# VectorE adds a chunk's residuals before it takes the pair output of the same round

## The chip, the cores and the metric

The kernel runs on one core of a Trainium2 chip. The metric is the device time of one execution in microseconds (us). The engines have short names in the profile: PE is TensorE (PEld its weight load), DVE is VectorE, ACT is ScalarE, POOL is GpSimd, SP is the engine whose queue issues the DMAs.

## What is computed

32 images of 512 channels and 48 x 48 pixels pass through two layers with residuals. Cut to what matters:

```
f     = relu(Wc @ gn(x) + bc)                  # 512 -> 128 channels       (stage A)
dynW  = kernels made per image from means and maxima of gn(x)
y     = conv3x3(f, dynW[n]) + b_ad             # 128 -> 128 channels       (stage B)
x1    = x + (Wf @ y + bf)                      # 128 -> 512 channels       (stage C)
out   = x1 + grouped_conv3x3(gn(x1), kernels)  # 32 groups of 16 channels  (stage D)
```

`gn` normalizes each of 32 groups of 16 channels. All products are made from a high and a low part of each operand, as three matmuls (`high*high`, `high*low`, `low*high`; lines 853, 854, 855).

## The kernel before, in words

Every engine runs its own list of instructions, in an order written out by hand, and semaphores tie the lists together. The unit of the lists is the step: one image n, for which stages A, B and C run, together with stage D of the image before, n - 1. Image 0 has no D beside it, and after image 31 the D of the last image runs alone. Images 2 to 29 run in a loop.

In a step TensorE makes stage A (tile `pac`), then stage B (`pb`), and then 16 rounds, r = 0 to 15. In each round it makes one pair of groups of D (`d_pair`: 18 matmuls into `pd` for even r, into `pb` for odd r). In rounds 0, 4, 8 and 11 (`C_AT`) it then makes one chunk of C: 128 of the 512 channels, as six units (`c_unit`) of three matmuls, each unit into one of three PSUM banks of `pac`. Between some rounds stand small matmuls for the statistics of the next image: the group mean (L908) behind round 7, the group variance (L912) behind round 9, and the inputs of the dynamic kernels (L920) behind round 11. The release rules of TensorE that the change touches are two lines:

```
if u >= C_BANKS: pe.wait_ge(x1_done, n * CUNITS + u - C_BANKS + 1)    # c_unit u: residual u - 3 is done
reached(pe, out_done, n * PAIRS + p - 1)                              # d_pair p: output p - 2 is taken
```

VectorE has two operations that read these results. `residual` (L764, one for each unit, writes `x1b`) adds bias and x to a unit and so frees its bank; with its sum it is two instructions, the main one and a DVE_READ_ACCUMULATOR. `output` (L774, one for each pair, writes `big`) scales the pair and adds x1. The first residual of a chunk also waits until the chunk before has been written out (`x1_out`) and until ScalarE has squared it (`sq_done`, L464), since `x1b` holds one chunk. In between VectorE works on the next image: moments (L604) in rounds 3 and 4, maxima (L612) in round 5, means (L622, L624) in round 6, variances (L630 to L638) in round 8, scales and scaled weights (L650 to L655) in round 10, their high and low parts (L659, L661) in round 11.

SP stores a quarter of an image's result once four outputs are there: `store` of chunk c of D waits for output 4c + 3, so that of chunk 2 waits for output 11. In the SP queue it stands ahead of the write of C's chunk 3 and of a load of x.

Of the kernel before, what the change touches and what calls it, by code (L numbers as in the profile page):

```python
# [81 lines left out]
def x_slot(c, odd):  # L82

    return c if c < 1 else c + 3 * odd
# [12 lines left out]
def build(nc, x, wct, bc, kks_in, wrow_in, b_ad, wft, bf, kt, out):  # L97
# [7 lines left out]
    with ExitStack() as ctx:  # L105
# [142 lines left out]
        def t_slot(c):  # L248
            return tb[:, T_SLOT[c], :, :, :]
# [9 lines left out]
        def pair_banks(p):  # L259

            return pb if p % 2 else pd


        def reached(eng, semaphore, value):

            if not isinstance(value, int) or value > 0:
                eng.wait_ge(semaphore, value)
# [273 lines left out]
        def _(vec):  # L541
# [135 lines left out]
            def x1_group_means(n):  # L677

                vec.wait_ge(stat_mm2, 2 * n + 1)
                reached(vec, behind_out, n * 16)  # L680
                reached(vec, ahead_out, n * 16)
                vec.tensor_scalar(mrow[:, :, :], ps[:, 32:32 + Q].unsqueeze(2).to_broadcast([P, Q, W]), -1.0, None,
                                  ALU.mult).then_inc(mrow_done, 1)
                vec.tensor_tensor(vb[:, 1, :], ps[:, 32:32 + Q], nmean[:, :], ALU.subtract).then_inc(dve_stat, 1)
                vec.wait_ge(dve_stat, STAT_LINKS * n + 2)
                vec.tensor_tensor(vb[:, 2, :], vb[:, 1, :], vb[:, 1, :], ALU.mult).then_inc(dve_stat, 1)

                vec.wait_ge(cen_done, (n + 1) * Q)
                vec.tensor_tensor(vb[:, 3, :], cen[:, :], nmean[:, :], ALU.subtract).then_inc(dve_stat, 1)
                vec.wait_ge(dve_stat, STAT_LINKS * n + 4)  # L690
                vec.tensor_tensor(vb[:, 3, :], vb[:, 3, :], vb[:, 3, :], ALU.mult).then_inc(dve_stat, 1)
                vec.wait_ge(dve_stat, STAT_LINKS * n + 5)
                vec.tensor_tensor(vb[:, 2, :], vb[:, 2, :], vb[:, 3, :], ALU.subtract).then_inc(dve_stat, 1)

            def x1_variances(n):

                vec.wait_ge(sq_done, (n + 1) * Q)
                vec.wait_ge(dve_stat, STAT_LINKS * n + 6)
                vec.scalar_tensor_tensor(out=vb[:, 0, :], in0=m2[:, :], scalar=1.0 / PX, in1=vb[:, 2, :],
                                         op0=ALU.mult, op1=ALU.add).then_inc(var_done, 1)  # L700
                vec.wait_ge(var_done, n + 1)
                mask = ind8[:, :].unsqueeze(1).to_broadcast([P, Q, GQ])
                vec.tensor_tensor(spread[:, 0], nmean[:, :].unsqueeze(2).to_broadcast([P, Q, GQ]), mask, ALU.mult)
                vec.tensor_tensor(spread[:, 1], vb[:, 0, :].unsqueeze(2).to_broadcast([P, Q, GQ]), mask,
                                  ALU.mult).then_inc(stat_ready2, 1)
# [24 lines left out]
            def x_low(n, odd, i):  # L730
                t, c = divmod(i, Q)
                r0, nr = TILES[t]
                vec.wait_ge(xs_hi, n * UNITS + i + 1)
                vec.scalar_tensor_tensor(out=xs_at(1, i, nr * W), in0=xb[:, x_slot(c, odd), r0 * W:(r0 + nr) * W],  # L734
                                         scalar=negm[:, c:c + 1], in1=f32(xs_at(0, i, nr * W)),
                                         op0=ALU.add, op1=ALU.subtract).then_inc(xs_lo, 1)

            def f_low(n, t):
                r0, nr = TILES[t]
                vec.wait_ge(f_hi, n * NT + t + 1)  # L740
                if t == 0:
                    reached(vec, sq_done, n * Q)
                vec.scalar_tensor_tensor(out=fl[:, r0 + 1:r0 + 1 + nr, 1:W + 1],
                                         in0=pac[:, t % 2, 0:nr * W].rearrange("p (r w) -> p r w", w=W), scalar=0.0,
                                         in1=f32(fh[:, r0 + 1:r0 + 1 + nr, 1:W + 1]), op0=ALU.max,
                                         op1=ALU.subtract).then_inc(f_lo, 1)
# [7 lines left out]
            def residual(n, odd, u):  # L754

                c, k = divmod(u, OR_)
                if k == 0:
                    if c == 0:
                        reached(vec, x1_out[Q - 1], n * 16)
                    else:  # L760
                        vec.wait_ge(x1_out[c - 1], (n + 1) * 16)
                    reached(vec, sq_done, n * Q + c)
                vec.wait_ge(c_mm, n * CUNITS + u + 1)
                vec.scalar_tensor_tensor(  # L764
                    out=x1b[:, c % X1_SLOTS, k, :].rearrange("p (b w) -> p b w", w=W),
                    in0=pac[:, u % C_BANKS, 0:BW].rearrange("p (b w) -> p b w", w=W), scalar=bfc[:, c:c + 1],
                    in1=xb[:, x_slot(c, odd), :].rearrange("p (b k w) -> p k b w", k=OR_, w=W)[:, k],
                    op0=ALU.add, op1=ALU.add, accum_out=sums[:, c, k:k + 1]).then_inc(x1_done, 1)

            def output(n, p):  # L770
                vec.wait_ge(d_mm, n * G + 2 * (p + 1))
                at = 2 * p % GQ
                dst = t_slot(p // PER_CHUNK)[0:M6, at:at + 2].rearrange("p j b w -> p j (b w)")
                vec.scalar_tensor_tensor(out=dst, in0=pair_banks(p)[0:M6, :, 0:BW], scalar=kout[0:M6, 2:3], in1=dst,  # L774
                                         op0=ALU.mult, op1=ALU.add).then_inc(out_done, 1)

            def step(n, odd, d=True, more=True):
                for t in range(NT):
                    for i in range(t * Q, (t + 1) * Q):
                        if i >= AHEAD:  # L780
                            x_low(n, odd, i)
                    if t:
                        f_low(n, t - 1)
                f_low(n, NT - 1)
                if d:
                    x1_group_means(n - 1)
                    x1_variances(n - 1)
                y_low(n, 0)
                for t in range(1, NT):
                    if t == SCALES_BEFORE and d:  # L790
                        for i in range(SCALE_STEPS):
                            x1_scales(n - 1, i)
                    if more and t <= len(STATS_IN_B):
                        moments(n + 1, 1 - odd, STATS_IN_B[t - 1])
                        maxima(n + 1, 1 - odd, STATS_IN_B[t - 1])
                    y_low(n, t)
                for r in range(PAIRS):
                    if d:
                        output(n - 1, r)
                    if r in C_AT:  # L800
                        for u in range(C_AT[r] * OR_, (C_AT[r] + 1) * OR_):
                            residual(n, odd, u)
                    if more and r in MOMENTS_AT:
                        c, part = MOMENTS_AT[r]
                        moments(n + 1, 1 - odd, c, range(part * BANDS, (part + 1) * BANDS))
                    if more and r in MAXIMA_AT:
                        maxima(n + 1, 1 - odd, MAXIMA_AT[r])
                    if more:
                        if r == PREP_MEANS_AT:
                            prep_means(n + 1)  # L810
                        if r == PREP_VARIANCES_AT:
                            prep_variances(n + 1)
                    if r == X1_SUMS_AT:
                        x1_means(n)
                    if more:
                        if r == PREP_SCALED_AT:
                            prep_scaled(n + 1, 0)
                            prep_scaled(n + 1, 1)
                        if r == PREP_SCALED_AT + 1:
                            prep_scaled(n + 1, 2)  # L820
                        for i in X_LOW_AT.get(r, ()):
                            x_low(n + 1, 1 - odd, i)
                        if r == DYN_LOW_AT:
                            dyn_low(n + 1)
# [204 lines left out]
```

## Time and profile before

| | |
|---|---|
| median of 3 runs | 3608.88 us (3607.25 to 3609.89) |
| profiled execution, its own time | 3609.87 us |
| its span, first to last instruction | 3608.1 us |
| PE busy | 3491.4 us, 97% |
| PEld busy | 2787.4 us, 77% |
| DVE busy | 2531.3 us, 70% |
| ACT busy | 2108.8 us, 58% |
| POOL busy | 965.9 us, 27% |
| DMA | mean 185 GB/s |

Busy time is a share of the span. A matmul's duration in the trace is longer than the distance to the next one, since matmuls are pipelined; the pace of TensorE is read from the start times. The chain of work tells which engine the end of the program waited for, step by step.

### The profile page before, as it was taken

To read this page: it belongs to the slowest core of one execution; us is meant where nothing else is said; L and a number is where in the kernel's file an instruction comes from. 1 tells how busy PE (TensorE), PEld (TensorE's weight loads), DVE (VectorE), ACT (ScalarE), POOL (GpSimd) and SP (SyncE) were. 2 spreads that over 40 slices of the span, in tenths; PEclk is the share of its full clock that TensorE was granted. 3 is DMA by queue.
4 is the path that set the end of the run, shared out by engine and by line. 5 is a ranking of instruction groups with operands and counts; after the bars stand their busy time and mean duration, and the time that the engine had idled before them with its cause. 6 is when DMAs were issued, how large, how long until landed. Compare 5 with 4: busy or idle time off the path is not lost.

```text
span 3608.1 us, 60228 instructions
## 1 busy us (share of the span) xinstructions
PE 3491.4 (97%) x18688; PEld 2787.4 (77%) x18688; DVE 2531.3 (70%) x5365; ACT 2108.8 (58%) x3559; POOL 965.9 (27%) x1039
## 2 busy tenths in 40 slices
PE   5799999999999999999999999999999999999996
PEld 4677877777877778877778777778777778777785
DVE  7666777776777777777677777767777767676642
ACT  4365555675555665655655556655556655556654
POOL 2033222232222232222332222332222322222323
PEclk9899999999999999999999999999999999999998
DMA  5567767677767677767677777677676677676666
GB/s 122 147 190 189 191 183 181 204 198 191 184 183 192 193 186 195 188 186 195 187 187 191 192 180 202 195 190 191 175 189 198 193 193 189 179 197 190 167 156 157
DMA packets 317577, 666.88 MB, mean 185 GB/s; under 512 B 58863, under 2 KB 288242, under 8 KB 288645
## 3 DMA queue, kind: packets, MB, share of 16 engines
q1 hardware_dynamic: 317317, 663.34, 68.9%
q8 instruction: 172, 2.82, 0.3%
q14 instruction: 88, 0.72, 0.1%
HBM read 355.00 MB, written 308.28 MB: 184 GB/s over the span
## 4 chain that ended last, share of the span: by engine, by line
PE 88%; issue 6%; DVE 4%; DMA 1%; DVEq 0%; POOL 0%; ACT 0%; SPq 0%; POOLq 0%; ACTq 0%
PE pb L853 15%; PE pb L855 15%; PE pb L854 15%; PE pd L853 7%; PE pd L855 7%; PE pd L854 7%; PE pac L853 7%; PE pac L854 6%; PE pac L855 6%; PE pac L927 2%; DVE x1b L764 1%; PE pac L862 1%; PE ps L920 1%; DMA big<-x 0%; DVE big L774 0%
## 5 line engine op out<-in xcount | busy, mean ns | idle before, releaser
L407 POOL TENSOR_TENSOR hl<-un,hl 128x384 f16<-128x384 f32 x1024 | 938.3, 916 | 2562.9 <-ACT hl L432 2559.8
L432 ACT ACTIVATE hl<-un 128x384 f16<-128x384 f32 x1024 | 539.1, 526 | 433.3 <-PE pb L855 363.2
L428 ACT ACTIVATE un<-big,b_t,s_t 128x384 f32<-128x384 f32 x1024 | 709.8, 693 | 15.4 <-DMA big<-x_rows 15.4
L853 PE MATMUL pb<-fh,dynh 128*128 128x480 f32 (+3 forms) x1440 | 543.7, 378 | 0.0
L854 PE MATMUL pb<-fl,dynh 128*128 128x480 f32 (+3 forms) x1440 | 541.0, 376 | 0.0
L855 PE MATMUL pb<-fh,dynl 128*128 128x480 f32 (+3 forms) x1440 | 540.7, 375 | 0.0
L774 DVE SCALAR_TENSOR_TENSOR big<-pd,kout,big 96x768 f32<-96x768 f32 x256 | 258.8, 1011 | 383.8 <-PE pd L855 383.8
L853 PE MATMUL pd<-hl,k_h 128*96 128x376 f16 (+1 forms) x1536 | 508.9, 331 | 18.1 <-POOL hl L407 18.1
L774 DVE SCALAR_TENSOR_TENSOR big<-pb,kout,big 96x768 f32<-96x768 f32 x256 | 258.8, 1011 | 355.1 <-PE pb L855 355.1
L854 PE MATMUL pd<-hl,k_h 128*96 128x376 f16 (+1 forms) x1536 | 506.7, 330 | 0.0
L853 PE MATMUL pb<-hl,k_h 128*96 128x376 f16 (+1 forms) x1536 | 506.7, 330 | 0.0
L855 PE MATMUL pd<-hl,k_l 128*96 128x376 f16 (+1 forms) x1536 | 506.6, 330 | 0.0
L855 PE MATMUL pb<-hl,k_l 128*96 128x376 f16 (+1 forms) x1536 | 505.8, 329 | 0.0
L854 PE MATMUL pb<-hl,k_h 128*96 128x376 f16 (+1 forms) x1536 | 505.7, 329 | 0.0
L454 ACT ACTIVATE xs<-pb,badc 128x480 fp32r<-128x480 f32 (+1 forms) x160 | 103.4, 646 | 658.8 <-PE pb L855 658.8
L442 ACT ACTIVATE xs<-big,negm 128x480 fp32r<-128x480 f32 (+1 forms) x640 | 397.0, 672 | 82.1 <-PE pac L855 81.0
L734 DVE SCALAR_TENSOR_TENSOR xs<-big,negm,xs 128x480 fp32r<-128x480 f32 (+1 forms) x640 | 436.4, 734 | 9.7 <-ACT xs L442 9.7
L764 DVE SCALAR_TENSOR_TENSOR x1b<-pac,bfc,big 128x384 f32<-128x384 f32 x768 | 422.4, 607 | 6.4 <-PE pac L855 6.0
L604 DVE BATCH_NORM_STATS2 bst<-big 128x6 f32<-128x384 f32 x768 | 367.3, 543 | 9.5 <-DMA big<-x 9.5
L612 DVE TENSOR_REDUCE mx<-big 128x3 f32<-128x768 f32 x384 | 339.8, 939 | 0.0
L853 PE MATMUL pac<-xs,wfh 128*128 128x384 f32 x768 | 295.6, 385 | 37.2 <-DVE x1b L764 28.7
L855 PEld LDWEIGHTS pb<-fh,dynl 128*128 128x128 f32 x1440 | 271.0, 188 | 41.7
(115 smaller groups left out, 5243.4 us busy)
## 6 DMA issues: line engine op xcount, KB each, us to landing
big<-x SPq DMA_DIRECT2D x128, 1152.0 KB, 9.8
x_rows<-x1b SPq DMA_DIRECT2D x128, 1152.0 KB, 5.6
big<-x_rows SPq DMA_DIRECT2D x128, 1152.0 KB, 12.6
out<-big SPq DMA_DIRECT2D x128, 1152.0 KB, 6.2
big<-x_rows SPq DMA_DIRECT2D x256, 192.0 KB, 13.1
x_rows<-mrow SPq DMA_DIRECT2D x64, 96.0 KB, 1.9
big<-kt SPq DMA_DIRECT2D x4, 288.0 KB, 10.7
big<-kt SPq DMA_DIRECT2D x2, 192.0 KB, 11.1
```

What stands on the lines that cost most here:

```text
L407: pool.tensor_tensor(hl[:, g % HL_RING, 1, :, 1:W + 1], un[:, g % U_RING], hl[:, g % HL_RING, 0, :, 1:W + 1], ALU.subtract).then_inc(hl_lo, 1)
L428: act.activation(un[:, g % U_RING], t_slot(g // GQ)[:, g % GQ], ACT.Identity, bias=b_t[:, g:g + 1], scale=s_t[:, g:g + 1]).then_inc(u_done, 1)
L432: act.activation(hl[:, g % HL_RING, 0, :, 1:W + 1], un[:, g % U_RING], ACT.Copy).then_inc(hl_hi, 1)
L442: act.activation(xs_at(0, i, nr * W), xb[:, x_slot(c, odd), r0 * W:(r0 + nr) * W], ACT.Identity, bias=negm[:, c:c + 1]).then_inc(xs_hi, 1)
L604: ins = vec.bn_stats(bst[:, c, i, :], xb[:, x_slot(c, odd), i * HALF:(i + 1) * HALF])
L612: ins = vec.tensor_reduce(mx[:, c, 3 * band:3 * band + 3], src.rearrange("p (r l w) -> p l r w", r=CELL, l=3), AX.XY, ALU.max)
L734: vec.scalar_tensor_tensor(out=xs_at(1, i, nr * W), in0=xb[:, x_slot(c, odd), r0 * W:(r0 + nr) * W], scalar=negm[:, c:c + 1], in1=f32(xs_a ...
L764: vec.scalar_tensor_tensor(out=x1b[:, c % X1_SLOTS, k, :].rearrange("p (b w) -> p b w", w=W), in0=pac[:, u % C_BANKS, 0:BW].rearrange("p ( ...
L774: vec.scalar_tensor_tensor(out=dst, in0=pair_banks(p)[0:M6, :, 0:BW], scalar=kout[0:M6, 2:3], in1=dst, op0=ALU.mult, op1=ALU.add).then_inc ...
L853: pe.matmul(acc, high_w, high_x, start=start, stop=False)
L854: pe.matmul(acc, high_w, low_x, start=False, stop=False)
L855: return pe.matmul(acc, low_w, high_x, start=False, stop=stop)
```

## The change

The two blocks of VectorE's rounds change places. In rounds 0, 4, 8 and 11 VectorE now does the six residuals of the chunk first and the output of the pair behind them. In the other rounds nothing changes, and the lists of TensorE, ScalarE, GpSimd and SP are the same as before.

```
                 for r in range(PAIRS):
-                    if d:
-                        output(n - 1, r)
                     if r in C_AT:
                         for u in range(C_AT[r] * OR_, (C_AT[r] + 1) * OR_):
                             residual(n, odd, u)
+                    if d:
+                        output(n - 1, r)
                     if more and r in MOMENTS_AT:
```

The first place is VectorE in round 11, behind the scaled weights (`wcs`) of round 10. `x1b<-pac` is a residual, `big<-pb` and `big<-pd` are outputs.

```order
 L598 SCALAR_TENSOR_TENSOR va<-va 128x4
 L655 TENSOR_TENSOR wcs<-wc,va 128x512
-L774 SCALAR_TENSOR_TENSOR big<-pb,kout,big 96x768
-L764 SCALAR_TENSOR_TENSOR x1b,sums<-pac,bfc,big 128x384 x6
+L764 SCALAR_TENSOR_TENSOR x1b,sums<-pac,bfc,big 128x384 x6
+L774 SCALAR_TENSOR_TENSOR big<-pb,kout,big 96x768
 L659 CAST wch<-wcs 128x512
 L661 TENSOR_TENSOR wcl<-wcs,wch 128x512
```

Output 11 has moved behind the six residuals of chunk 3; the high and low weights behind them stay where they were.

The second place is VectorE from round 3 to round 6, with the chunk of round 4 and the statistics behind it. Before:

```order
L604 BN_STATS bst<-big 128x6 x3
L774 SCALAR_TENSOR_TENSOR big<-pd,kout,big 96x768
L764 SCALAR_TENSOR_TENSOR x1b,sums<-pac,bfc,big 128x384 x6
L604 BN_STATS bst<-big 128x6 x3
L774 SCALAR_TENSOR_TENSOR big<-pb,kout,big 96x768
L612 TENSOR_REDUCE mx<-big 128x3 x3
L774 SCALAR_TENSOR_TENSOR big<-pd,kout,big 96x768
L622 COPY cent<-mx 128x4x9
L624 BN_AGGR mv<-bst 128x2 x4
```

And with the change:

```order
L604 BN_STATS bst<-big 128x6 x3
L764 SCALAR_TENSOR_TENSOR x1b,sums<-pac,bfc,big 128x384 x6
L774 SCALAR_TENSOR_TENSOR big<-pd,kout,big 96x768
L604 BN_STATS bst<-big 128x6 x3
L774 SCALAR_TENSOR_TENSOR big<-pb,kout,big 96x768
L612 TENSOR_REDUCE mx<-big 128x3 x3
L774 SCALAR_TENSOR_TENSOR big<-pd,kout,big 96x768
L622 COPY cent<-mx 128x4x9
L624 BN_AGGR mv<-bst 128x2 x4
```

Output 4 now stands behind the residuals and ahead of the moments of round 4; everything from there on keeps its order. Rounds 0 and 8 change in the same way.

## Rows read from the trace of the kernel before

**Rows 1.** The page: span, TensorE, and granted clock in 40 slices

```profile
span 3608.1 us, 60228 instructions
...
PE 3491.4 (97%) x18688; PEld 2787.4 (77%) x18688; DVE 2531.3 (70%) x5365; ACT 2108.8 (58%) x3559; POOL 965.9 (27%) x1039
...
PEclk9899999999999999999999999999999999999998
```

**Rows 2.** The page: chain that ended last, by engine

```profile
PE 88%; issue 6%; DVE 4%; DMA 1%; DVEq 0%; POOL 0%; ACT 0%; SPq 0%; POOLq 0%; ACTq 0%
```

**Rows 3.** Waits between 130 and 3420 us: total us, times, longest us

```profile
PEld pac L853 <- DVE x1b L764: 62.7, 120, 2.9
...
PE pac L853 <- DVE x1b L764: 19.1, 32, 2.6
```

**Rows 4.** Timeline, chunk of round 0, image 14: start us, us, instruction

```profile
1610.64 0.47 PE L853 MATMUL pac<-xs,wfh 128*128 128x384 f32 x1
...
1610.98 1.01 DVE L774 SCALAR_TENSOR_TENSOR big<-pd,kout,big 96x768 f32<-96x768 f32 x1 [1.75 <-PE pd L855]
...
1611.12 0.34 PE L855 MATMUL pac<-xs,wfl 128*128 128x384 f32 x1
...
1611.83 0.34 PE L853 MATMUL pac<-xs,wfh 128*128 128x384 f32 x1
...
1611.91 0.60 DVE L764 SCALAR_TENSOR_TENSOR x1b<-pac,bfc,big 128x384 f32<-128x384 f32 x1
...
1612.45 0.61 DVE L764 SCALAR_TENSOR_TENSOR x1b<-pac,bfc,big 128x384 f32<-128x384 f32 x1
...
1612.58 0.19 PEld L853 LDWEIGHTS pac<-xs,wfh 128*128 128x128 f32 x1 [0.38 <-DVE x1b L764]
...
1613.21 0.34 PE L853 MATMUL pac<-xs,wfh 128*128 128x384 f32 x1
...
1614.29 0.33 PE L853 MATMUL pb<-hl,k_h 128*96 128x384 f16 x1
...
1617.26 0.33 PE L853 MATMUL pd<-hl,k_h 128*96 128x384 f16 x1
```

**Rows 5.** Timeline, chunk of round 11, image 14

```profile
1653.90 1.27 DVE L655 TENSOR_TENSOR wcs<-wc,va 128x512 f32<-128x512 f32 x1
...
1654.28 0.47 PE L853 MATMUL pac<-xs,wfh 128*128 128x384 f32 x1
...
1655.10 1.00 DVE L774 SCALAR_TENSOR_TENSOR big<-pb,kout,big 96x768 f32<-96x768 f32 x1
...
1655.46 0.34 PE L853 MATMUL pac<-xs,wfh 128*128 128x384 f32 x1
...
1656.02 0.60 DVE L764 SCALAR_TENSOR_TENSOR x1b<-pac,bfc,big 128x384 f32<-128x384 f32 x1
...
1656.69 0.19 PEld L853 LDWEIGHTS pac<-xs,wfh 128*128 128x128 f32 x1 [0.86 <-DVE x1b L764]
```

**Rows 6.** Timeline, chunk of round 0, image 30, and the next pair

```profile
3361.55 0.45 PE L853 MATMUL pac<-xs,wfh 128*128 128x384 f32 x1 [1.79 <-DVE xs L751]
...
3362.48 0.62 DVE L764 SCALAR_TENSOR_TENSOR x1b<-pac,bfc,big 128x384 f32<-128x384 f32 x1
...
3364.86 0.33 PE L853 MATMUL pb<-hl,k_h 128*96 128x384 f16 x1
```

**Rows 7.** Timeline, rounds 4 to 7, image 14

```profile
1626.41 1.01 DVE L774 SCALAR_TENSOR_TENSOR big<-pd,kout,big 96x768 f32<-96x768 f32 x1 [0.58 <-PE pd L855]
...
1632.91 1.01 DVE L774 SCALAR_TENSOR_TENSOR big<-pb,kout,big 96x768 f32<-96x768 f32 x1 [0.87 <-PE pb L855]
...
1637.67 0.83 DVE L624 BATCH_NORM_AGGREGATE mv<-bst 128x2 f32<-128x36 f32 x4
...
1638.67 0.28 PE L908 MATMUL ps<-mv,ind 128*128 128x4 f32 x2
```

**Rows 8.** Timeline of ScalarE: the square between rounds 9 and 11, image 14

```profile
1647.71 2.23 ACT L464 ACTIVATE fl<-x1b,cen 128x2304 fp32r<-128x2304 f32 x1
```

More of the change, by code:

```diff
@@ L797, in step @@
                 for r in range(PAIRS):
-                    if d:
-                        output(n - 1, r)
                     if r in C_AT:
@@ L802, in step @@
                             residual(n, odd, u)
+                    if d:
+                        output(n - 1, r)
                     if more and r in MOMENTS_AT:
```

## The prediction

> **What bounds the kernel now.** I read the page first. TensorE is busy for 97% of the span, the granted clock stands in its upper tenths throughout [rows 1], and the chain that ended last is 88% TensorE, against 4% VectorE [rows 2]. So time taken from TensorE's list is time taken from the kernel, and a wait of VectorE costs only where TensorE waits for it. The list of waits then shows where it does: in the stretch that holds nearly all steps, the weight load in front of a unit of C waits for a residual 120 times, 62.7 us in all; the matmuls themselves show 19.1 us of that, 32 times, because a matmul still in flight covers the rest [rows 3].
>
> The timeline of one chunk shows how it comes about [rows 4]. Unit 0 starts at 1610.64. Its third matmul starts at 1611.12, lasts 0.34, and so ends at 1611.46. VectorE is then inside the output, from 1610.98, and starts the first residual only at 1611.91. Unit 3 needs that residual's bank. It starts at 1612.58, 0.67 after the residual's start, and the weight load shows 0.38 us of waiting. Unit 2 started at 1611.83, so the distance is 0.75. Unit 4 comes 0.63 later, with its own weight load no longer hidden, and the next pair starts at 1614.29: the chunk takes 3.65 us. In round 11 it is worse, for VectorE comes late to the output itself: it finishes the scaled weights, starts the output at 1655.10 and the first residual at 1656.02, and unit 3 stands at 1656.69, 1.23 behind unit 2 [rows 5].
>
> **What a chunk costs without the wait.** The trace has one such chunk. In image 30 unit 0 had itself waited, the first residual started 0.93 behind it, and no unit waited: 3361.55 to 3364.86 is 3.31 us [rows 6]. Unit 0 to unit 1 is 0.02 to 0.03 shorter there than behind a running pair, so I take 3.33 for the others, or 0.54 per unit in between.
>
> **The change part by part.** It removes nothing and adds nothing: the same 24 residuals and 16 outputs in each step. It moves four outputs behind six residuals each.
>
> First, rounds 0, 4 and 8. The first residual now waits only for its unit. The output started 0.04 after the end of the pair's last matmul (1610.61 + 0.33 = 10.94, and 10.98 [rows 4]); a residual with the same delay starts at 1611.50 instead of 1611.91. Unit 3 is released at 1611.50 + 0.67 = 1612.17, and its natural place is 1611.83 + 0.54 = 1612.37: no wait, with 0.20 to spare. The next residuals run 0.54 apart (1611.91 to 1612.45), as fast as the units. So a chunk goes from 3.65 to 3.33: 0.32 us.
>
> Second, round 11. VectorE is free at 1655.10 and unit 0 is done at 1654.28 + 0.82 = 1655.10 too; with the delay the residual starts at 1655.14, unit 3 is released at 1655.81, and its natural place is 1655.46 + 0.54 = 1656.00. Again no wait. Saved is the 0.32 of the other chunks plus the longer stall, 1.23 - 0.75 = 0.48: 0.80 us.
>
> Count: images 1 to 31 have 31 x 3 = 93 chunks of the first kind, less the one of image 30 that waits for nothing, plus the round 11 of image 31, which has no next image's statistics in front: 93 x 0.32 = 29.8. Round 11 of images 1 to 30: 30 x 0.80 = 24.0. Round 4 of image 1 has 0.5 us more of stall, which may stay. Sum 54 us; as a check, 3 x 0.38 + 0.86 = 2.00 us of weight-load waits in a step, 60 over 30 steps, is nearly the 62.7 of the view [rows 3], and it is more than my sum because 0.19 or so of each is hidden under the running matmuls and 0.10 comes back at unit 4.
>
> Third, the outputs come later, and who waits for them. Output r now starts when the last residual lets go: 0.86 + 6 x 0.54 = 4.10 after unit 0, and ends at 5.1. Pair r + 2 needs it and starts 3.33 + 2.97 = 6.30 after unit 0 (a pair takes 1617.26 - 1614.29 = 2.97 [rows 4]). It is hidden with 1.2 us to spare; without that cover it would cost its excess, 124 times. The store behind output 11 comes about 3 us later, and with it the write of C's chunk 3 and a load of x. The first reader of either stands in the next step, tens of microseconds away: nothing.
>
> Fourth, the statistics behind round 4, the tightest place. VectorE had 0.87 us of idle time before output 5 [rows 7]. The first residual starts 0.86 after unit 0 where the output started 0.34 after it, so the sequence up to the moments ends 0.52 later; and TensorE brings pair 5 0.32 earlier. 0.87 - 0.52 - 0.32 leaves 0.03. From output 5 on VectorE runs without a gap to the aggregate, which ends at 1637.67 + 0.83 = 1638.50, and TensorE's group mean starts at 1638.67 [rows 7]. So a lateness under about 0.1 us is swallowed, and I take zero. Were 0.2 us left over, it would be 6 us over 30 steps; that is a bound of the range.
>
> At TensorE's restart the Trainium skill can be weighed. The row shows that unit 3's weights are loaded only when the residual is done (weight load and release at 1612.58), and unit 4 comes 0.63 later, 0.09 over the natural distance [rows 4]. The Trainium skill, TensorE: Matmul & The Clock Gate, section "Step-by-step: what each phase is for", says that weight loads are pulled ahead of matmuls in flight, which would hide the load under the wait. By the row that 0.09 is in the saving; by the rule it would not be, and the gain would be 124 x 0.09 = 11 us less. The row decides, since load and matmul both stand behind the same wait here.
>
> **Sum.** The profiled execution's span of 3608.1 becomes 3554, its time of 3609.87 becomes 3556; it was 1.0 above the median of 3608.88. From the median: 3608.88 - 54 = 3555. Scatter between runs is 2.6 us, so 0.2% (7 us) is about what a measurement of this kernel can tell from no change.
>
> **The rivals.**
>
> (1) The waits go, but part comes back: a residue at the group mean (6 us), or residuals that pace units at 0.54 where TensorE alone could do 0.53 and a restart of 0.09 that stays in each chunk (11 us). For it: the margins of 0.20, 0.19 and 0.03 are small. Against it: the chunk of image 30 had its first residual 0.93 behind unit 0, later than the 0.86 here, and ran free [rows 6]. Time: 3555 + 6 to 17 = 3561 to 3572.
>
> (2) Three banks bind whatever the order, and the stall only moves to a later unit. This is also the reading of the Trainium skill, Perfetto Trace Analysis, section "Optimization Strategy": the same gap again and again on the engine that should be saturated can mean too few buffers. For it: the gap stands at the first unit that reuses a bank. It would hold if the first residual came more than 1.73 - 0.67 = 1.06 after unit 0; before it was 1.27 [rows 4], now 0.86, and image 30 had 0.93 without a gap. Time: 3609, no change; if in round 11 alone, since VectorE comes there late, 3555 + 24 = 3579.
>
> (3) Slower: the late output becomes TensorE's wait. Output r stands behind the chunk's first residual, which waits for the square of the chunk before and for its write. If that lasts, pair r + 2 stops. It takes 1.2 us of lateness to be felt and 1.2 + 54/124 = 1.6 us at every chunk to eat the gain; at 2.2 us it costs 124 us against 54, 3679. Against it: the square between rounds 9 and 11 ends at 1649.94 [rows 8], and the first residual of round 11 starts at 1655.1: 5 us to spare. Only an output kept back by something that the trace does not show would do it.
>
> **How the numbers follow.** Gain as summed: 0.80, with its own range 3550 to 3561 (scatter of 2.6 us, and the 0.01 or 0.02 us by which a chunk can be misread, 124 times). Rival 1: 0.11. Rival 2: 0.05, of which 0.02 for no change at all and 0.03 for round 11 alone. Rival 3: 0.02. Unnamed, either side: 0.02. The range takes in the first two: 3549 to 3569. Faster by over 0.2%: 0.80 + 0.11 + 0.03 = 0.94, and 0.01 of the unnamed; same 0.02; slower 0.03.
>
> **What would show it.** In the waits, weight loads of `pac` behind `x1b` fall from 62.7 us to a few. In the timeline, a chunk takes 3.33 us in all four rounds of a step, the first residual starts 0.86 behind unit 0, and the output starts at 4.1. The step gets 1.76 us shorter. TensorE shows no wait for L774. The aggregate still ends before the group mean's place. The prediction is wrong if unit 3 still waits, if a wait before a pair or before L908 appears, or if a step shortens by less than 1.4 us.

## The result, and the profile after

The kernel with the change takes 3551.47 us (median of 4 runs, 3549.79 to 3554.75) against 3608.23 us (4 runs, 3607.25 to 3609.89): 56.8 us less, a ratio of 0.9843 with a 95% interval of 0.9826 to 0.9860.

The page of the profiled execution, which was the fastest of the four:

```profile
span 3548.0 us, 60228 instructions
...
PE 3453.4 (97%) x18688; PEld 2804.6 (79%) x18688; DVE 2551.1 (72%) x5365; ACT 2108.9 (59%) x3559; POOL 966.6 (27%) x1039
...
PE 97%; DVE 1%; DMA 1%; issue 0%; POOL 0%; ACT 0%; SPq 0%; POOLq 0%; ACTq 0%
```

In the last line, the chain that ended last, the 6% of "issue" and 3 of the 4% of VectorE of [rows 2] are gone, and 97% is TensorE. The busy share of TensorE says nothing: it was 97% before and is 97% now, because matmuls that overlap in the trace hide waits of a few tenths of a us.

The waits between 130 and 3370 us, first TensorE's weight loads, then VectorE (total, times, longest):

```profile
PEld pac L853 <- DVE x1b L764: 2.9, 1, 2.9
```

```profile
DVE x1b L764 <- PE pac L855: 179.0, 89, 2.8
```

Against 62.7 us in 120 waits [rows 3], one wait is left. It stands at 130.46 in image 0, whose step has no outputs that could move; in images 1 to 31 no unit of C waits for a residual. VectorE's own waits have moved with its order. It now waits in front of the first residual of 89 chunks, for 2.0 us each, and less often in front of an output. Before (130 to 3420 us), then after (130 to 3370 us):

```profile
DVE big L774 <- PE pd L855: 332.6, 178, 2.6
DVE big L774 <- PE pb L855: 323.4, 180, 3.9
```

```profile
DVE big L774 <- PE pb L855: 229.2, 120, 3.9
DVE big L774 <- PE pd L855: 172.0, 90, 2.1
```

With the 179.0 us in front of residuals that is 580 us, where it was 656. VectorE waits less in all, not more.

The chunk of round 0 in image 14, to be laid beside [rows 4]:

```profile
1584.46 0.47 PE L853 MATMUL pac<-xs,wfh 128*128 128x384 f32 x1
...
1584.94 0.34 PE L855 MATMUL pac<-xs,wfl 128*128 128x384 f32 x1
...
1585.32 0.62 DVE L764 SCALAR_TENSOR_TENSOR x1b<-pac,bfc,big 128x384 f32<-128x384 f32 x1 [2.28 <-PE pac L855]
...
1585.65 0.34 PE L853 MATMUL pac<-xs,wfh 128*128 128x384 f32 x1
...
1586.18 0.34 PE L853 MATMUL pac<-xs,wfh 128*128 128x384 f32 x1
...
1587.76 0.33 PE L853 MATMUL pb<-hl,k_h 128*96 128x384 f16 x1
...
1588.56 1.01 DVE L774 SCALAR_TENSOR_TENSOR big<-pd,kout,big 96x768 f32<-96x768 f32 x1
...
1590.74 0.33 PE L853 MATMUL pd<-hl,k_h 128*96 128x384 f16 x1
```

The residual starts 0.86 after unit 0, unit 3 comes 0.53 behind unit 2 (0.75 before), and the chunk takes 3.30 us. The output starts at 4.10 and ends at 5.11, the pair that needs it starts at 6.28. In round 11, beside [rows 5]:

```profile
1626.66 1.28 DVE L655 TENSOR_TENSOR wcs<-wc,va 128x512 f32<-128x512 f32 x1
...
1627.05 0.47 PE L853 MATMUL pac<-xs,wfh 128*128 128x384 f32 x1
...
1627.90 0.62 DVE L764 SCALAR_TENSOR_TENSOR x1b<-pac,bfc,big 128x384 f32<-128x384 f32 x1
...
1628.24 0.34 PE L853 MATMUL pac<-xs,wfh 128*128 128x384 f32 x1
1628.44 0.08 DVE L764 DVE_READ_ACCUMULATOR x1b<-pac,bfc,big 128x1 f32 x1
...
1628.77 0.33 PE L853 MATMUL pac<-xs,wfh 128*128 128x384 f32 x1
```

Unit 3 stands 0.53 behind unit 2, where it stood 1.23 behind it.

### The profile page after: what moved, and what is told of

The parts are those of the page before. It is cut to its first block, busy times and chain, and to the rows that moved or that the text cites. A ratio compares the mean times of both kernels' runs of the same rounds, so it can differ in the third digit from the quotient of the medians.

```text
span 3548.0 us, 60228 instructions
## 1 busy us (share of the span) xinstructions
PE 3453.4 (97%) x18688; PEld 2804.6 (79%) x18688; DVE 2551.1 (72%) x5365; ACT 2108.9 (59%) x3559; POOL 966.6 (27%) x1039
## 4 chain that ended last, share of the span: by engine, by line
PE 97%; DVE 1%; DMA 1%; issue 0%; POOL 0%; ACT 0%; SPq 0%; POOLq 0%; ACTq 0%
PE pb L853 16%; PE pb L854 16%; PE pb L855 16%; PE pac L853 8%; PE pac L854 8%; PE pac L855 8%; PE pd L853 7%; PE pd L855 7%; PE pd L854 7%; PE pac L927 2%; PE pac L862 1%; PE ps L920 1%; DVE bst L604 0%; DVE mx L612 0%; PE ps L921 0%
## 5 line engine op out<-in xcount | busy, mean ns | idle before, releaser
L854 PEld LDWEIGHTS pb<-fl,dynh 128*128 128x128 f32 x1440 | 271.2, 188 | 39.6
```

What stands on the lines that cost most here:

```text
L854: pe.matmul(acc, high_w, low_x, start=False, stop=False)
```

## The experiments

All edits are to VectorE's list, except the one on banks. The kernel before was run beside each group; its medians there were 3607.2, 3608.9 and 3606.5 us.

### The two parts alone

`e1_round11` puts the residuals first in round 11 alone, `e2_rounds048` in rounds 0, 4 and 8 alone:

```
+                    if d and r not in (11,):        # or (0, 4, 8)
+                        output(n - 1, r)
                     if r in C_AT: ... residual(n, odd, u)
-                    if d:
+                    if d and r in (11,):            # or (0, 4, 8)
                         output(n - 1, r)
```

> Residuals first in round 11 alone; rounds 0, 4 and 8 take the output first, as before. Theory (each chunk pays for itself, through the bank that unit 3 waits for): the chunk of round 11 goes from 4.21 to 3.39 us in images 1 to 30, the others stay at 3.65, so 3608 - 25 = 3583 us. Rival (the stall of round 11 is VectorE being late over the whole step, and the gain needs all rounds): less than 12 us of gain. Rival (three banks bind anyway): no change.

> The other part: residuals first in rounds 0, 4 and 8, output first in round 11. Theory: 92 chunks go from 3.65 to 3.30 us, 3608 - 32 = 3576 us, and together with the other part the 57 us of the whole change. Rival (the parts are not independent): the two gains do not add up to 57 within 4 us.

Measured: 3583.34 us for round 11 (ratio 0.9934, 0.9920 to 0.9948), a gain of 23.9; 3574.96 us for the other three (0.9909, 0.9894 to 0.9925), a gain of 32.3. The sum is 56.1 us, and the whole change brought 56.8. The parts add up, so each chunk pays for itself, and the rival of a lateness that builds up over the step is out.

### Where in the chunk the output stands

The output goes behind the third, the second or the first residual of its chunk:

```
-                        for u in range(C_AT[r] * OR_, (C_AT[r] + 1) * OR_):
-                            residual(n, odd, u)
+                    for u in units[:3]:              # or 2, or 1
+                        residual(n, odd, u)
                     if d:
                         output(n - 1, r)
+                    for u in units[3:]:
+                        residual(n, odd, u)
```

> All four rounds: three residuals, the output, three residuals. Theory (what counts is only that the residuals for which units 3, 4 and 5 wait, the first three, come ahead of the output): no unit waits, chunks 3.30 us, 3551 us, equal to the change. Rival (a residual behind the output is late whatever its number, or the last residual's time counts): at least a part of the 0.35 us of each chunk comes back, 3560 to 3608 us.

> All four rounds: two residuals, the output, four residuals. Theory: the third residual starts at 0.86 + 2 x 0.54 + 0.93 = 2.87 us after unit 0, unit 5 is released 0.67 later, at 3.54, and would have started at 2.78; with the restart of 0.09 a chunk takes 4.15 us, 124 chunks x 0.85 = 105 us more than the change: 3656 us, slower than the kernel before although two residuals are ahead of the output. Rival (the further back the output stands, the better): between the kernel before and the change, 3551 to 3608 us.

> All four rounds: one residual, the output, five residuals. Theory: the second residual starts at 0.86 + 0.54 + 0.93 = 2.33 us after unit 0, unit 4 is released at 3.00 and would have started at 2.25; with the restart of 0.09 a chunk takes 4.14 us, 0.84 more than in the change, 124 times: 3655 us. Rival (the further back the output stands, the better): between the kernel before and the change, 3551 to 3608 us, and nearer to the kernel before than with two residuals ahead.

Measured: 3551.51 us behind the third (ratio 0.9845, 0.9831 to 0.9858), 3659.63 us behind the second (1.0148, 1.0132 to 1.0163), 3659.53 us behind the first (1.0142, 1.0126 to 1.0159). The step between two and three is 108 us. It is the sharpest test of the cause: TensorE's unit u waits for residual u - 3, a chunk has six units, so only the first three residuals are waited for within the chunk. The chunk of round 4 with the output behind the second residual (this kernel's matmul lines are two higher):

```profile
1645.16 0.47 PE L855 MATMUL pac<-xs,wfh 128*128 128x384 f32 x1
...
1647.11 1.01 DVE L774 SCALAR_TENSOR_TENSOR big<-pd,kout,big 96x768 f32<-96x768 f32 x1
...
1648.04 0.60 DVE L764 SCALAR_TENSOR_TENSOR x1b<-pac,bfc,big 128x384 f32<-128x384 f32 x1
...
1648.71 0.19 PEld L855 LDWEIGHTS pac<-xs,wfh 128*128 128x128 f32 x1 [0.93 <-DVE x1b L764]
...
1649.33 0.33 PE L855 MATMUL pb<-hl,k_h 128*96 128x384 f16 x1
```

The third residual starts at 2.88 after unit 0 and unit 5 at 3.55; the chunk takes 4.17 us. So an output between residuals can cost more than one in front of all: in front, a part of its 0.93 us lies beside the running units 0 to 2.

### Two banks

```
-                if u >= C_BANKS:
-                    pe.wait_ge(x1_done, n * CUNITS + u - C_BANKS + 1)
+                if u >= UNIT_BANKS:                  # 2; also in the bank index of unit and residual
+                    pe.wait_ge(x1_done, n * CUNITS + u - UNIT_BANKS + 1)
```

> The change, but the units of C use two PSUM banks in turn, not three. Theory (a bank is busy for 0.86 us until its residual starts and 0.67 more until the next unit may, 1.51 to 1.53 in all): unit 2 and unit 4 wait, a chunk takes 4.2 us, 0.9 more, 124 times: 3663 us; the order alone is not enough, it needs the three banks. Rival (with the residuals first the bank count no longer matters): 3551 us.

Measured: 3671.42 us (ratio 1.0175, 1.0158 to 1.0192), 120 us more than the change. The order alone is not enough. A bank is taken for 1.54 us from one unit to the next one in it (units 0, 2 and 4 start at 1654.43, 1655.97 and 1657.48 in one chunk), which three units at 0.53 (1.59) just cover and two do not. The chunks of images 1 to 31 took 116 of the 120 us; the expectation of 3663 had put a chunk at 4.2 us, and it took 4.24. So with three banks the order decides, and with two the banks bind. The opposite remedy, a fourth bank with the old order, was not tried; `pac`, `pb`, `pd` and `ps` hold 3, 2, 2 and 1 banks in this kernel, so it needs one more. As an estimate from [rows 4], unit 4 would then wait for the first residual, until 1612.58, and its natural place was 1612.91: the wait of rounds 0, 4 and 8 would be gone by that too.

### How late an output may be

Starting from the change, output 4 goes further back: behind the moments of round 4, and then also behind one, two or all three instructions of the maxima of round 5. In these last three output 5 moves along behind it; no wait for output 5 shows in their traces.

```
-                    if d:
+                    if d and r != 4:                 # for the later places: r not in (4, 5)
                         output(n - 1, r)
                     ... moments of round 4 ...
+                    if d and r == 4:                 # for the later places, in round 5, behind
+                        output(n - 1, r)             # 1, 2 or 3 maxima: output 4, then output 5
```

> The change, with output 4 put one step further back, behind the moments of round 4. Theory (a late output is free until pair r + 2 wants to start): the output ends 6.58 us after unit 0, pair 6 would start at 6.27, so it waits 0.36, with the restart 0.4 us, in 30 images: 3563 us. Rival (late outputs already cost something in the change, one for one): the full 1.47 us, 30 times: 3596 us. Rival (nobody waits for an output): 3551 us.

> The change, with output 4 behind the moments of round 4 and the maxima of round 5. Theory: the output ends at 9.16 us after unit 0, pair 6 would start at 6.27, it waits 2.9 us, 30 times: 3641 us, slower than the kernel before; a wait for L774 in front of pd stands in the trace. Rival (nobody waits for an output): 3551 us. Rival (one for one from the start): 1.47 + 2.58 = 4.05 us, 30 times: 3673 us.

> The change, with output 4 behind the moments of round 4 and one of the three maxima of round 5. Theory of the wait alone: 1.20 us, 30 times: 3587 us, granted clock at 1.0 in every step. Rival (a fixed excess): 3620 us.

> The change, with output 4 behind the moments of round 4 and two of the three maxima of round 5. Theory of the wait alone (0.86 us less than behind all three, where a step without a clock fall lost 2.92 us): 2.06 us, 30 times: 3613 us, with the granted clock at 1.0 in every step. Rival (the excess of the run with three maxima over 3641 us is a fixed cost of any late output, not the clock): 3613 + 33 = 3646 us.

Measured, against the 3551.5 us of the change:

| output 4 behind | expected | measured | ratio to the kernel before |
|---|---|---|---|
| moments | 3563 | 3563.79 | 0.9876 (0.9860 to 0.9893) |
| and 1 maximum | 3587 | 3591.31 | 0.9958 (0.9943 to 0.9974) |
| and 2 maxima | 3613 | 3624.65 | 1.0047 (1.0032 to 1.0063) |
| and 3 maxima | 3641 | 3674.72 | 1.0181 (1.0164 to 1.0198) |

The first two bear out that a late output is free up to the start of pair r + 2 and then costs its excess: 1.4 us of delay cost 0.4 us a step. With one maximum the median step is 1.22 us longer, which gives 37 of the 40 us; the other 3 us are not placed. The list of waits doesn't say so. In the run with the moments alone it puts pair 6's wait down to GpSimd:

```profile
1609.48 1.00 DVE L774 SCALAR_TENSOR_TENSOR big<-pd,kout,big 96x768 f32<-96x768 f32 x1
...
1609.64 0.89 POOL L407 TENSOR_TENSOR hl<-un,hl 128x384 f16<-128x384 f32 x1 [3.67 <-ACT hl L432]
...
1610.60 0.12 PEld L855 LDWEIGHTS pd<-hl,k_h 128*96 128x96 f16 x1 [0.54 <-POOL hl L407]
```

The pair waits for both engines' semaphores, and these two instructions end 0.05 us apart, at 1610.48 and 1610.53. GpSimd's is for a later pair, since it runs groups ahead of TensorE; only the output had moved. With two and three maxima the time goes 12 and 34 us over the sum of waits. The rival of a fixed excess is out too (3646 us with two maxima, 3620 with one). The trace of the last run shows where the excess comes from. Two steps around the late output, TensorE's first matmuls of pair 6 (lines three higher in this kernel):

```profile
1660.26 0.33 PE L856 MATMUL pb<-hl,k_h 128*96 128x376 f16 x1
...
1663.67 0.36 PE L856 MATMUL pd<-hl,k_h 128*96 128x384 f16 x1 [2.75 <-DVE big L774]
...
1664.21 0.33 PE L856 MATMUL pd<-hl,k_h 128*96 128x376 f16 x1
...
1664.70 0.33 PE L856 MATMUL pd<-hl,k_h 128*96 128x376 f16 x1
...
1774.07 0.36 PE L856 MATMUL pd<-hl,k_h 128*96 128x384 f16 x1 [2.75 <-DVE big L774]
...
1774.61 0.33 PE L856 MATMUL pd<-hl,k_h 128*96 128x376 f16 x1
...
1775.36 0.52 PE L856 MATMUL pd<-hl,k_h 128*96 128x376 f16 x1
...
1776.32 0.52 PE L856 MATMUL pd<-hl,k_h 128*96 128x384 f16 x1
```

Both steps wait 2.75 us. After the first the sets of three matmuls keep their pace of 0.49 to 0.54; after the second they come 0.75 and then 0.96 apart. The windows of the same two steps show the granted clock (the number in front of the DMA share):

```profile
1665.00:1670.00 5.00, 5.00 (x34) 3.79 (x32) 2.48 (x7) 3.44 (x7) 2.67 (x3) 1.00 1.11 208
...
1773.00:1778.00 5.00, 3.93 (x15) 2.55 (x16) 1.86 (x3) 2.73 (x5) 1.67 (x2) 0.68 1.03 234
```

The granted clock is 1.00 in the first and 0.68 in the second, a mean of 2.4 and 1.2 GHz: it fell behind that idle time and rose again within the pair. The trace's record of the clock has such falls in 22 of the 30 steps with three maxima (wait 2.75 us), in 7 with two (1.9 us, where a clock of 1.0 in every step had been expected), and in none with one (1.0 us) or with the moments alone. Pair 6 takes 3.01 us in every step without a fall and 4.51 to 4.66 in those with one, so a fall costs up to 1.65 us: 22 times that is 36 us and 7 times is 12, against the 34 and 12 us over the sum.

### How tight the statistics are

One more moments instruction (0.5 us, into an unused tile) in round 4 of each step, once on top of the change and once on top of the kernel before:

```
+                if parts[0] == BANDS:
+                    vec.bn_stats(spare[:, :], xb[:, x_slot(c, odd), 0:HALF])
                 for i in parts:
                     ins = vec.bn_stats(bst[:, c, i, :], ...)
```

> The change, with one more moments instruction (half a us, into a tile that nobody reads) in round 4 of each step. Theory (the change has used up VectorE's idle time before output 5, so anything more there reaches the group mean behind round 7): the aggregate ends 0.49 us later, TensorE waits 0.4 to 0.55 us in front of the group mean, in 30 steps: 12 to 16 us, 3563 to 3568 us. Rival (VectorE, busy for 72%, has room): 3551 us.

> The same moments instruction more, in the kernel before. Theory (there the idle time of 0.87 us before output 5 takes it up): no change, 3608 us. Rival (the place was as tight before the change): 12 to 16 us more, 3620 to 3624 us.

Measured: on the kernel before 3607.78 us against 3606.47 (ratio 1.0004, 0.9995 to 1.0013), no difference, and the idle time before output 5 is 0.40 us there; on the change 3557.44 us (0.9862 to the kernel before), 6 us more than the change, not 12 to 16. So the direction holds: the 0.87 us of idle time before output 5 [rows 7] used to take such work up and the change has spent it. The size does not. Where the rest went is in the traces, around the copy in front of the aggregate. First the change as it is, then with the added instruction (its lines are one to three higher):

```profile
1609.94 0.89 POOL L407 TENSOR_TENSOR hl<-un,hl 128x384 f16<-128x384 f32 x1 [0.27 <-ACT hl L432]
1610.46 0.41 DVE L622 COPY cent<-mx 128x36 f32<-128x36 f32 x1
1610.79 0.83 DVE L624 BATCH_NORM_AGGREGATE mv<-bst 128x2 f32<-128x36 f32 x4
...
1611.68 0.30 PEld L908 LDWEIGHTS ps<-mv,ind 128*128 128x128 f32 x2
```

```profile
1614.80 0.90 POOL L408 TENSOR_TENSOR hl<-un,hl 128x384 f16<-128x384 f32 x1 [0.26 <-ACT hl L433]
1615.69 0.17 DVE L625 COPY cent<-mx 128x36 f32<-128x36 f32 x1
1615.78 0.83 DVE L627 BATCH_NORM_AGGREGATE mv<-bst 128x2 f32<-128x36 f32 x4
...
1616.66 0.30 PEld L911 LDWEIGHTS ps<-mv,ind 128*128 128x128 f32 x2 [0.22 <-DVE mv L627]
```

In the change the copy starts while GpSimd's subtraction runs (to 1610.83) and lasts 0.41 us, to 1610.87. With the added work it starts at 1615.69, when that subtraction has just ended (1615.70), and lasts 0.17. So 0.24 us of the lateness is time that the copy would have spent anyway. Counted from unit 0 of the same chunk of round 4 (1599.54, then 1604.40), the copy starts 0.37 us later with the added 0.46 us of work, since some 0.09 was left before output 5, and the weight load of the group mean only 0.12 later. Its 0.22 us of idle time is not all new: in the change it was 0.09, too little for the view to print. The median step grows by the same 0.12 us, and the 30 steps together by 4.9; in the profiled runs another 2.7 us lie ahead of image 1's first chunk, which the added work does not explain. The Trainium skill, SBUF — State Buffer, section "SBUF: two separate sides", says that VectorE and GpSimd share one port pair as an exclusive lock, which a GpSimd instruction holds to its end against a VectorE instruction in a mode that uses both ports. An fp32 copy within SBUF is one of those by its warning on DMAs in the same section. That fits the two rows; that it is this lock was not tried apart.

## Why the prediction was right

**The bound and the saving.** TensorE's list was the kernel, and the sum over chunks is the whole result. In images 1 to 31 the chunks of rounds 0, 4 and 8 went from 3.65 to 3.31 us on average, those of round 11 from 4.21 to 3.39 in images 1 to 30. Added up over all 124 chunks that is 32.1 us for the first kind and 24.8 for round 11, together 56.9, against 56.8 between the medians. The forecast was 54, because it took 3.33 for a chunk without a wait from the one in image 30 [rows 6] with 0.02 added; the others were shorter than that, 3.30. It is the term that was mis-sized, by 0.02 us, 123 times, or 2.5 us. The rest is the 0.5 us of longer stall in round 4 of image 1, which the prediction let stay and which went. The span of the profiled execution fell by 60 us, more than the medians; 2.4 us of that lie ahead of the first chunk that the change touches (unit 0 of image 1 starts at 186.88, before at 189.31), where the granted clock between 130 and 170 us is 0.91 on average and was 0.87.

**The margins.** The first residual started 0.86 after unit 0, as worked out, and unit 3 did not wait. The 0.09 us of the restart at unit 4 is gone with the wait (0.63 before, 0.53 now), as the row said. That does not contradict the rule that the prediction weighed against it (the Trainium skill, TensorE: Matmul & The Clock Gate, section "Step-by-step: what each phase is for"). Where no unit waits, the trace agrees with it: unit 2's weight load starts at 1585.48 and its matmul at 1585.65. The rule speaks of matmuls in flight; that a load would also pass a wait for a semaphore was the prediction's reading of it, and the 11 us that it weighed rested on that reading. The outputs are 1.2 us ahead of their use, and the runs with a later output found the edge close to where the prediction put it: 1.37 us later cost 0.33, so it is nearer to 1.05, since the pair starts 0.13 behind the end of the output that it waits for. VectorE's idle time before output 5 went to some 0.1 us or less, and the group mean waited no longer than before; that place has some 0.24 us more room than was worked out, from the copy.

**The rivals.** "Part comes back" did not happen. "Three banks bind whatever the order" was wrong for three and right for two. "Slower through late outputs" is real as a mechanism, and begins near where it was put; what the prediction missed of it is that with waits of 1.9 us in some steps, and of 2.75 us in most, the granted clock made it dearer than the wait.

## What to carry to other kernels

When an in-order engine has two results to take and the producer is about to reuse the bank of one of them, that one goes first; the other may wait until its own reader is due. Count how many of the first kind are waited for (here three of six), and put the second kind behind exactly these or later, never among them. New idle time of the consumer, 2.0 us in front of each first residual here, is no loss if the producer's waits vanish. But the room in front of output 5 is spent (0.87 us before), and the next work added there shows.

## What the runs showed of the hardware

With a wait of 2.75 us before a pair TensorE's granted clock fell to 1.2 GHz in 22 of 30 steps, with one of 1.9 us in 7, with one of 1.0 us in none; a fall cost up to 1.65 us beyond the wait. A 128 x 36 copy on VectorE took 0.17 us when it began at the end of a GpSimd instruction, and 0.41 when it began in the middle of one, ending 0.04 us behind it.
